# An 8-head attention phase inside a four-phase decoder kernel: one row tile turned before the scores, the keys made in halves, and another order of weight copies in the last batch

## The chip, the cores and the metric

The kernel runs on one core of one Trainium2 chip. The metric is device time in microseconds (us) of one execution; lower is better. The kernel before takes 1964.75 us, the median of 3 runs (1964.06 to 1965.6).

## The reference, cut to what matters

Sixteen sequences of 256 rows with 512 features go through four phases: 16-head cross attention, a ternary gated FFN, 8-head cross attention, a routed FFN. The change is in the third phase. For each of the 16 batches it computes, with the normalised x (normalised twice: once without and once with gain and bias):

```python
q = xn @ Wq ; k, v = split(media @ Wkv)       # 512 -> 8 heads of 64
sim = q k^T / 8, masked ; attn = softmax(sim)
x = x + (attn @ v) @ Wo
```

Everything is float32 in the reference. The kernel multiplies in three terms: each operand is a high part (rounded) and a low part (the rest), and hi*hi, lo*hi and hi*lo are added up in PSUM.

## The kernel before, in words

One program runs the four phases (tags a, b, c, m) one behind the other on five engines: TensorE (PE), ScalarE (ACT), VectorE (DVE), GpSimd (POOL) and the DMA queue of SyncE. Each engine follows an order written out by hand, and semaphores that count finished pieces tie the engines together. No planner sets it: an instruction waits behind all that stand ahead of it on its engine.

`attention_phase` serves phases a (16 heads, QUADS = 4) and c (8 heads, QUADS = 2). Phase c runs from about 1022 to 1608 us of the span. A quad is four heads, so a batch `el` has two quads, q = 0 and q = 1. In iteration `el`, quad q, TensorE (`tensor`, loop at L1212) does for j = 0 to 3:

- only at j = 0: `scores` of the next quad (24 matmuls, L1151), then `probs_v` of the quad before (16 matmuls, L1183);
- `transpose_probs` of head j (4 transposes into one shared bank, L1168), whose result is copied to SBUF by DVE for even j (`probs_out`, L877) and by ACT for odd j (L683); a transpose waits for the copy of the head before it;
- `use_slot`: the units listed in `SLOTS[q][j]` (L247). A unit makes one tile of the next batch, or the output rows of the batch before: `tx0`, `tx1` turn the two tiles of 128 normalised rows (4 transposes each, L1088), `k0`, `k1`, `q0`, `q1` make two feature groups of keys or queries (24 matmuls of 256 columns, L1112; "k0a" and "k0b" are its halves of 12), `v0`, `v1` make 128 rows of values, and `o0`, `o1` the output rows (L1098).

Units alternate between two PSUM banks (`UnitOrder.bank`). `tx0`, `k0` and `o0` use the one, `tx1` and `q0` the other. Before a unit writes its bank (`bank_free`), the unit before it in that bank must be read: ACT copies the high part out of the bank (`hi_of`, for tx at L623), then DVE subtracts it from the bank to get the low part (`lo_of`, for tx at L832). So `k0` waits until DVE has finished `tx0`. The keys come from the stored context and don't need `tx`; `q0` needs both `tx`.

ACT and DVE run `quad_of_8` (L748 and L987): ACT the exponentials of the next quad (`exps`, L675), DVE the scaled and masked scores out of PSUM (`scores_out`, L868), the reciprocals and the norm of the even heads (`recip`, L884 and L890), both the parts of the units slot by slot (`hi_of_slot`, `lo_of_slot`). POOL norms the odd heads and normalises x for the batch after next (`normalise`, L514), whose row tiles `tx0` and `tx1` of one iteration later take as input. In the first iteration that normalise is still running (its rows are below).

In the last batch there is no next batch, and the slots hold work of phase m instead (`beside`): TensorE turns 12 pieces of the shared expert weights (L2557), 2 at a time in quad 0 in slots 0, 1, 2, and 3 at a time in quad 1 in slots 0 and 1; ACT copies the high part of each (`scalar_slot`, L2212), DVE subtracts the low part (`vector_slot`, L2320). A turn waits for the low part of an earlier one that used its bank; `o0` of quad 0, slot 3, waits for the fifth low part. In slots 2 and 3 of quad 1 TensorE turns the first rows of phase m (L2525), after all twelve low parts.

Of the kernel before, what the change touches and what calls it, by code (L numbers as in the profile page):

```python
# [145 lines left out]
def attention_phase(nc, ctx, banks, tag, heads, x_in, ctx_in, mask_in, mask_value, x_out, w_views, q_bias, k_bias,  # L146
# [6 lines left out]
    QUADS = heads // 4  # L153
# [87 lines left out]
    if QUADS == 4:  # L241
        SLOTS = [[["tc0"], ["o0a"], ["o0b"], ["tc1", "o1a", "o1b"]],
                 [["tx0", "v0a"], ["v0b"], ["tx1", "k0a"], ["k0b"]],
                 [["q0a"], ["q0b"], ["v1a"], ["v1b"]],
                 [["k1a"], ["k1b"], ["q1a"], ["q1b"]]]
    else:
        SLOTS = [[["tx0", "tx1"], ["k0a", "k0b"], ["q0a", "q0b"], ["o0a", "o0b"]],  # L247
                 [["o1a", "o1b"], ["k1a", "k1b"], ["q1a", "q1b", "v0a"], ["v0b", "v1a", "v1b"]]]
    BEHIND = ("o0", "o1")
    POOL_NORMS_EVEN = QUADS == 4  # L250

    def finished(parts):

# [11 lines left out]
    def last_batch(el):  # L265
        return isinstance(el.n, int) and el.n == batches - 1
# [11 lines left out]
    def owner(el, u):  # L278

        return el.plus(units.offset(u))  # L280

    def exists(el, u):

        n = el.n
        return not isinstance(n, int) or 0 <= n + units.offset(u) < batches
# [374 lines left out]
    def scalar(act, beside=None):  # L660

        def hi_of_slot(el, q, j):
            for u in finished(SLOTS[q][j]):
                if exists(el, u):
                    hi_of(act, owner(el, u), u)
            if beside and QUADS == 2 and quads_left(el, q):
                beside.scalar_slot(act, quads_left(el, q), j)

        def exps(el, q, h):

            s = slot_of(q, h)
            for t in range(QT):
                act.wait_ge(ttr_done, (el.n * heads + 4 * q + h) * QT + t + 1)
                pr = probs[:, s, h % 2, t]
                nc.scalar.activation(pr, pr, ACT.Exp, bias=negm[:, s, h % 2, t:t + 1], scale=-1.0,  # L675
                                     accum_out=ssum[:, s, QT * (h % 2) + t:QT * (h % 2) + t + 1]) \
                    .then_inc(exp_done, 1)

        def probs_out(el, q, j):

            h = 4 * q + j
            act.wait_ge(pt_done, el.n * heads + h + 1)
            nc.scalar.activation(pT[:, (h // hpg) % 2, h % hpg].rearrange("p t n -> p (t n)"),  # L683
                                 pt_bank[:], ACT.Copy).then_inc(odd_out, 1)

        def attn_hi(el, q):

            act.wait_ge(pv_done, quads_upto(el, q))
            rows = oT[el.par % OT_SETS][:, HI, q * GPQ:(q + 1) * GPQ].rearrange("p g n -> p (g n)")
            if v_bias is None:  # L690
                nc.scalar.activation(rows, o_bank[:, 0:GPQ * SEQ], ACT.Copy).then_inc(othi_done, 1)
            else:
                nc.scalar.activation(rows, o_bank[:, 0:SEQ], ACT.Identity, bias=cols[:, BV, q:q + 1]).then_inc(othi_done, 1)

        def attn_hi_before(el, q):
            if q > 0 or has_before(el):
                attn_hi(*quad_before(el, q))

        start = Element(0, 0, batches)
        if prior:  # L700
            hi_of(act, start, "q0")
            hi_of(act, start, "v0")
            exps(start, 0, 0)
            exps(start, 0, 1)
            hi_of(act, start, "k1")
            exps(start, 0, 2)
            exps(start, 0, 3)
            hi_of(act, start, "q1")
            hi_of(act, start, "v1")
        else:  # L710
            hi_of(act, start, "tc0")
            hi_of(act, start, "tc1")
            hi_of_weight(act, "Wk")
            hi_of(act, start, "tx0")
            hi_of(act, start, "tx1")
            hi_of_weight(act, "Wq")
            hi_of(act, start, "k0")
            hi_of_weight(act, "Wv")
            hi_of(act, start, "k1")
            hi_of(act, start, "q0")  # L720
            hi_of_weight(act, "Wo")
            hi_of(act, start, "v0")
            exps(start, 0, 0)
            exps(start, 0, 1)
            hi_of(act, start, "v1")
            exps(start, 0, 2)
            exps(start, 0, 3)
            hi_of(act, start, "q1")

        def quad_of_16(el, q):  # L730
            ne, nq = next_quad(el, q)
            more = nq > 0 or el.has(1)
            if more:
                exps(ne, nq, 0)
            attn_hi_before(el, q)
            hi_of_slot(el, q, 0)
            probs_out(el, q, 1)
            if more:
                exps(ne, nq, 1)
            hi_of_slot(el, q, 1)  # L740
            if more:
                exps(ne, nq, 2)
            hi_of_slot(el, q, 2)
            probs_out(el, q, 3)
            if more:
                exps(ne, nq, 3)
            hi_of_slot(el, q, 3)

        def quad_of_8(el, q):
            ne, nq = next_quad(el, q)  # L750
            more = nq > 0 or el.has(1)
            if more:
                exps(ne, nq, 0)
            attn_hi_before(el, q)
            if q > 0 and more:
                exps(ne, nq, 1)
            hi_of_slot(el, q, 0)
            probs_out(el, q, 1)
            if q == 0 and more:
                exps(ne, nq, 1)  # L760
            if more:
                exps(ne, nq, 2)
            hi_of_slot(el, q, 1)
            if more:
                exps(ne, nq, 3)
            hi_of_slot(el, q, 2)
            probs_out(el, q, 3)
            hi_of_slot(el, q, 3)

        def iteration(el):  # L770
            for q in range(QUADS):
                (quad_of_16 if QUADS == 4 else quad_of_8)(el, q)
                if beside and quads_left(el, q):
                    beside.scalar_beside(act, quads_left(el, q))

        run_elements(act, batches, iteration)
        attn_hi(Element(0, batches - 1, batches), QUADS - 1)
# [25 lines left out]
    def mask_bias(dve, el):  # L803

        dve.wait_ge(m_loaded[el.par], el.dma())
        nc.vector.tensor_scalar(mbias[:, el.par], mraw[:, el.par], 0.0, mask_value,
                                ALU.is_equal, ALU.mult).then_inc(mbias_ready, 1)
# [53 lines left out]
    def vector(dve, beside=None):  # L861
# [30 lines left out]

        def lo_of_slot(el, q, j):
            for u in finished(SLOTS[q][j]):
                if exists(el, u):
                    lo_of(dve, owner(el, u), u)
            if beside and QUADS == 2 and quads_left(el, q):
                beside.vector_slot(dve, quads_left(el, q), j)
# [90 lines left out]
        def quad_of_8(el, q):  # L989
            ne, nq = next_quad(el, q)  # L990
            more = nq > 0 or el.has(1)
            if q > 0:
                lo_of_slot(el, q - 1, 3)
            elif has_before(el):
                lo_of_slot(el.plus(-1), QUADS - 1, 3)
            if more:
                scores_out(ne, nq, 0)
                scores_out(ne, nq, 1)
                scores_out(ne, nq, 2)
            probs_out(el, q, 0)  # L1000
            if q == 0:
                lo_of_slot(el, q, 0)
            attn_lo_before(el, q)
            if more:
                scores_out(ne, nq, 3)
            if q > 0:
                lo_of_slot(el, q, 0)
            if q == 0 and el.has(1):
                mask_bias(dve, el.plus(1))
            if more:  # L1010
                recip(ne, nq, 0)
            probs_out(el, q, 2)
            lo_of_slot(el, q, 1)
            lo_of_slot(el, q, 2)
            if more:
                recip(ne, nq, 1)
            if q == 0 and el.has(2):
                row_stats(dve, el.plus(2))
# [114 lines left out]
    def tensor(pe, beside=None):  # L1133

        def use_slot(el, q, j):
            for u in SLOTS[q][j]:
                name = u.rstrip("ab")
                if exists(el, name):
                    use(pe, owner(el, name), u)

        def scores(el, q):
# [70 lines left out]
        def iteration(el):  # L1212
            for q in range(QUADS):
                ne, nq = next_quad(el, q)
                for j in range(4):
                    if j == 0 and QUADS == 2:
                        if nq > 0 or el.has(1):
                            scores(ne, nq)
                        probs_v_before(el, q)
# [1615 lines left out]
```

## Time and profile before

| what | value |
|---|---|
| median of 3 runs | 1964.75 us |
| the profiled execution | 1968.88 us, span 1967.2 us |
| TensorE busy | 1904.2 us, 97% of the span |
| VectorE busy | 1296.6 us, 66% |
| ScalarE busy | 1032.7 us, 52% |
| GpSimd busy | 788.1 us, 40% |
| chain that ended last | PE 89%, DVE 3%, issue 2% |
| phase c, time of one batch in the loop | 35.1 us |

The profile shows one execution. Busy is the time in which an engine had an instruction running; for TensorE the ends of matmuls are modelled, so that starts are the surer measure. In a timeline row the first number is the start, the second the busy time of the merged group, and a bracket gives the idle time ahead of it and what ended it. PEclk is the clock granted to TensorE as a share of 2.4 GHz (0.50 is 1.2 GHz).

### The profile page before, as it was taken

To read this page: it belongs to the slowest core of one execution; us is meant where nothing else is said; L and a number is where in the kernel's file an instruction comes from. 1 tells how busy PE (TensorE), PEld (TensorE's weight loads), DVE (VectorE), ACT (ScalarE), POOL (GpSimd) and SP (SyncE) were. 2 spreads that over 40 slices of the span, in tenths; PEclk is the share of its full clock that TensorE was granted. 3 is DMA by queue.
4 is the path that set the end of the run, shared out by engine and by line. 5 is a ranking of instruction groups with operands and counts; after the bars stand their busy time and mean duration, and the time that the engine had idled before them with its cause. 6 is when DMAs were issued, how large, how long until landed. Compare 5 with 4: busy or idle time off the path is not lost.

```text
span 1967.2 us, 43371 instructions
## 1 busy us (share of the span) xinstructions
PE 1904.2 (97%) x13796; PEld 1459.8 (74%) x13828; DVE 1296.6 (66%) x4001; ACT 1032.7 (52%) x2654; POOL 788.1 (40%) x1446
## 2 busy tenths in 40 slices
PE   6999999999999799999989999999999989999998
PEld 5888888888888544444448888888888867787875
DVE  5777777777776678888865655656556556544475
ACT  5777767776777744644435444444444433222252
POOL 2455445454545855655533221312213122222263
PEclk9999999999999999999999999999999989999999
DMA  6332234222325467756653122121221326321131
GB/s 214 121 134 84 83 103 146 83 83 93 136 100 197 141 152 194 184 129 142 148 120 123 56 87 76 65 97 54 86 76 65 103 85 213 103 87 65 64 129 44
DMA packets 197387, 219.54 MB, mean 112 GB/s; under 512 B 105456, under 2 KB 115696, under 8 KB 197248
## 3 DMA queue, kind: packets, MB, share of 16 engines
q1 hardware_dynamic: 197248, 217.93, 35.6%
q8 instruction: 57, 0.93, 0.2%
q14 instruction: 82, 0.67, 0.1%
HBM read 144.47 MB, written 50.35 MB: 99 GB/s over the span
## 4 chain that ended last, share of the span: by engine, by line
PE 89%; DVE 3%; issue 2%; DMA 1%; POOL 1%; ACT 1%; SPq 1%; POOLq 0%; DVEq 0%; ACTq 0%
PE bank L1112 19%; PE bank L1098 18%; PE bank L2619 13%; PE bank L1820 10%; PE bank L1168 8%; PE bank L1183 6%; PE bank L1835 6%; PE bank L1151 5%; PE bank L1088 2%; DMA b_hqT<-b_hq 1%; PE bank L2525 1%; DVE c_xnT L832 1%; SPq L1379 1%; PE bank L2658 1%; ACT c_xnT L623 0%
## 5 line engine op out<-in xcount | busy, mean ns | idle before, releaser
L550 POOL TENSOR_SCALAR a_probs<-a_probs,a_rinv 128x256 f32<-128x256 f32 x512 | 237.4, 482 | 302.6 <-DVE a_rinv L884 302.6
L675 ACT ACTIVATE a_probs<-a_probs,a_negm 128x256 f32<-128x256 f32 x512 | 254.6, 502 | 113.3 <-DVE a_negm L868 112.7
L550 POOL TENSOR_SCALAR c_probs<-c_probs,c_rinv 128x256 f32<-128x256 f32 x128 | 67.0, 533 | 384.6 <-DVE c_rinv L884 384.6
L868 DVE CUSTOM_DVE_ANT_0 a_probs<-bank,a_mbias 128x256 f32<-128x256 f32 x512 | 191.7, 417 | 6.0 <-PE bank L1151 4.3
L2619 PE MATMUL bank<-m_xnT,m_s 128*128 128x512 f32 x768 | 187.0, 395 | 2.7 <-DVE m_hid L2360 2.7
L877 DVE COPY a_pT<-bank 128x512 f32<-128x512 f32 x128 | 88.2, 689 | 137.0 <-PE bank L1168 136.8
L2619 PEld LDWEIGHTS bank<-m_xnT,m_s 128*128 128x128 f32 x768 | 144.2, 190 | 34.1 <-DVE m_hid L2360 3.3
L675 ACT ACTIVATE c_probs<-c_probs,c_negm 128x256 f32<-128x256 f32 x256 | 127.0, 500 | 72.1 <-DVE c_negm L868 72.1
L1168 PE MATMUL bank<-a_ident,a_probs 128*128 128x128 f32 x1024 | 155.2, 274 | 8.3 <-ACT a_pT L683 4.6
L1168 PEld LDWEIGHTS bank<-a_ident,a_probs 128*128 128x128 f32 x1024 | 122.0, 141 | 26.0 <-issue 8.6
L868 DVE CUSTOM_DVE_ANT_0 c_probs<-bank,c_mbias 128x256 f32<-128x256 f32 x256 | 92.8, 419 | 68.1 <-PE bank L1151 68.1
L1638 ACT ACTIVATE b_hq<-b_hround 128x1024 bf16<-128x1024 f32 x64 | 67.3, 1052 | 125.3 <-POOL b_hround L1565 121.3
L1820 PE MATMUL bank<-b_wg,b_xqT 128*128 128x512 bf16 x502 | 130.1, 379 | 1.5 <-issue 1.0
L1820 PE MATMUL bank<-b_wu,b_xqT 128*128 128x512 bf16 x503 | 130.1, 379 | 1.0 <-DVE b_hid L1734 0.5
L1835 PE MATMUL bank<-b_wd,b_hqT 128*128 128x512 bf16 x499 | 116.8, 383 | 7.5 <-DMA b_hqT<-b_hq 6.5
L2149 POOL TENSOR_TENSOR m_hidT<-m_hid,m_hidT 128x512 fp32r<-128x512 f32 x32 | 41.7, 1304 | 196.0 <-ACT m_hidT L2230 196.0
L683 ACT ACTIVATE a_pT<-bank 128x512 f32<-128x512 f32 x128 | 76.3, 596 | 71.0 <-PE bank L1168 70.2
L1624 ACT ACTIVATE b_gate<-bank,b_xs 128x512 f32<-128x512 f32 x128 | 87.0, 683 | 48.5 <-PE bank L1820 44.1
L1112 PE MATMUL bank<-a_cT,a_wk 128*128 128x256 f32 x768 | 109.2, 293 | 1.5 <-DVE a_wk L784 1.5
L1112 PE MATMUL bank<-a_xnT,a_wq 128*128 128x256 f32 x768 | 107.1, 289 | 0.0
L1734 DVE SCALAR_TENSOR_TENSOR b_hid<-bank,b_xs,b_gate 128x512 f32<-128x512 f32 x128 | 95.5, 747 | 16.1 <-ACT b_gate L1624 12.8
L1098 PE MATMUL bank<-a_wv,a_cT 128*128 128x512 f32 x384 | 104.0, 407 | 1.2 <-DVE a_wv L784 1.2
(284 smaller groups left out, 4341.7 us busy)
## 6 DMA issues: line engine op xcount, KB each, us to landing
kept<-a_cT SPq DMA_DIRECT2D x32, 512.0 KB, 5.4
m_ew<-in_L_ffn_w_dram SPq DMA_DIRECT2D x24, 512.0 KB, 8.6
a_cbuf<-in_ctx_dram SPq DMA_DIRECT2D x16, 512.0 KB, 6.4
a_xbuf<-in_x_dram SPq DMA_DIRECT2D x16, 512.0 KB, 5.8
a_resb<-in_x_dram SPq DMA_DIRECT2D x16, 512.0 KB, 4.2
x<-a_resb SPq DMA_DIRECT2D x16, 512.0 KB, 2.8
b_xbuf<-x SPq DMA_DIRECT2D x32, 256.0 KB, 2.9
b_resb<-x SPq DMA_DIRECT2D x32, 256.0 KB, 3.2
```

The source lines that it names most:

```text
L550: last = nc.gpsimd.tensor_scalar(pr, pr, rinv[:, s, r:r + 1], 0.0, ALU.mult, ALU.add)
L675: nc.scalar.activation(pr, pr, ACT.Exp, bias=negm[:, s, h % 2, t:t + 1], scale=-1.0, accum_out=ssum[:, s, QT * (h % 2) + t:QT * (h % 2) + ...
L868: nc.vector.tensor_tensor_reduce(out=probs[:, s, h % 2, t], in0=s_bank[h][:, t * SEQ:(t + 1) * SEQ], in1=mbias[:, el.par], scale=-sm_scale ...
L1098: last = nc.tensor.matmul(dst[:], src[:, t * P:(t + 1) * P], w[:, b, k], start=(k == 0 and (a, b) == TERMS[0]), stop=(k == KC - 1 and (a, ...
L1112: last = nc.tensor.matmul(dst[:, m * SEQ:(m + 1) * SEQ], w[:, b, k, f * P:(f + 1) * P], xnT[:, a, k] if u[0] == "q" else turned_context(el ...
L1151: last = nc.tensor.matmul(s_bank[h][:, t * SEQ:(t + 1) * SEQ], qT[el.par][r, a, f, t * P:(t + 1) * P], kT[el.par][r, b, f], start=((a, b) ...
L1168: last = nc.tensor.transpose(pt_bank[:, kt * SEQ + t * P:kt * SEQ + (t + 1) * P], probs[:, s, m, t, kt * P:(kt + 1) * P], ident[:])
L1183: last = nc.tensor.matmul(o_bank[c, i * SEQ:(i + 1) * SEQ], vb[:, el.par, kt, g * P + m * hd:g * P + (m + 1) * hd], pT[:, g % 2, m, kt], s ...
L1734: nc.vector.scalar_tensor_tensor(hid[:, el.par, c * DIM:(c + 1) * DIM], u_bank[c % 2][:], xs[:, el.par, 1:2], gate[:, c % 4], ALU.mult, AL ...
L1820: last = nc.tensor.matmul(bank[c % 2][:], xqT[:, el.par, k], w[:, k, c * DIM:(c + 1) * DIM], start=(k == 0), stop=(k == KC - 1))
L1835: last = nc.tensor.matmul(d_bank[:], hqT[:, el.par, k], wd[:, k], start=(k == 0), stop=(k == IK - 1))
L2619: ins = nc.tensor.matmul(bank[:], *operands(a, b, k), start=(k == 0 and (a, b) == TERMS[0]), stop=(k == KC - 1 and (a, b) == TERMS[-1]))
```

## The change

1. Slots: `k0a` moves from slot (0, 1) to slot (0, 0), behind `tx1`; so the transposes of head 1 now stand between the two halves of `k0`.
2. `tx0` leaves slot (0, 0): TensorE turns it ahead of the scores of the next quad, ACT copies its high part ahead of the first exponentials, DVE makes its low part ahead of the first scores. This is for every iteration of phase c that has a next batch (15 of 16).
3. In the last batch, ACT makes the high parts of slot 1 before `exps` of head 2 instead of behind it, and DVE makes the low parts of slot 1 before the reciprocals and the copy of head 2 instead of behind them, in both quads.

```diff
-        SLOTS = [[["tx0", "tx1"], ["k0a", "k0b"], ["q0a", "q0b"], ["o0a", "o0b"]],
+        SLOTS = [[["tx0", "tx1", "k0a"], ["k0b"], ["q0a", "q0b"], ["o0a", "o0b"]],
                  [["o1a", "o1b"], ["k1a", "k1b"], ["q1a", "q1b", "v0a"], ["v0b", "v1a", "v1b"]]]
+    AHEAD = "tx0" if QUADS == 2 else None
...
@@ hi_of_slot on ACT; the same in lo_of_slot on DVE and in use_slot on PE @@
-                if exists(el, u):
+                if exists(el, u) and u != AHEAD:
...
@@ quad_of_8 on ACT @@
+            if q == 0 and exists(el, AHEAD):
+                hi_of(act, owner(el, AHEAD), AHEAD)
             if more:
                 exps(ne, nq, 0)
             attn_hi_before(el, q)
...
             if q == 0 and more:
                 exps(ne, nq, 1)
+            if last_batch(el):
+                hi_of_slot(el, q, 1)
             if more:
                 exps(ne, nq, 2)
-            hi_of_slot(el, q, 1)
+            if not last_batch(el):
+                hi_of_slot(el, q, 1)
             if more:
                 exps(ne, nq, 3)
...
@@ quad_of_8 on DVE @@
+            if q == 0 and exists(el, AHEAD):
+                lo_of(dve, owner(el, AHEAD), AHEAD)
             if more:
                 scores_out(ne, nq, 0)
                 scores_out(ne, nq, 1)
...
+            if last_batch(el):
+                lo_of_slot(el, q, 1)
             if more:
                 recip(ne, nq, 0)
             probs_out(el, q, 2)
-            lo_of_slot(el, q, 1)
+            if not last_batch(el):
+                lo_of_slot(el, q, 1)
             lo_of_slot(el, q, 2)
...
@@ the loop over quads and heads on PE @@
+                    if j == 0 and q == 0 and QUADS == 2 and exists(el, AHEAD):
+                        use(pe, owner(el, AHEAD), AHEAD)
                     if j == 0 and QUADS == 2:
                         if nq > 0 or el.has(1):
                             scores(ne, nq)
```

## Rows read from the trace of the kernel before

**Rows 1.** Section 4 of the page: the chain that ended last, share of the span by engine.
```profile
PE 89%; DVE 3%; issue 2%; DMA 1%; POOL 1%; ACT 1%; SPq 1%; POOLq 0%; DVEq 0%; ACTq 0%
```

**Rows 2.** Windows: busy us of PE, PEld, DVE, ACT, POOL; PEclk, DMA, GB/s; one batch.
```profile
1252.80:1287.90 35.10, 34.67 (x267) 29.64 (x266) 20.52 (x65) 16.68 (x48) 8.48 (x19) 1.00 0.21 76
```

**Rows 3.** Waits of the phase (1030 to 1580): total us, times, longest.
```profile
PE bank L1112 <- DVE c_xnT L832: 5.8, 14, 0.4
```

**Rows 4.** Timeline of that batch, TensorE: start us, us, engine, line, count [idle before].
```profile
1252.82 1.69 PE L1151 MATMUL bank<-c_kT,c_qT 64*128 64x256 f32 x24
...
1256.32 0.66 PE L1168 MATMUL bank<-c_ident,c_probs 128*128 128x128 f32 x4
...
1256.81 1.04 PE L1088 MATMUL bank<-c_ident,c_xn 128*128 128x128 f32 x8
...
1257.85 0.63 PE L1168 MATMUL bank<-c_ident,c_probs 128*128 128x128 f32 x4
...
1258.90 3.13 PE L1112 MATMUL bank<-c_cT_odd,c_wk 128*128 128x256 f32 x24 [0.43 <-DVE c_xnT L832]
...
1261.87 0.60 PE L1168 MATMUL bank<-c_ident,c_probs 128*128 128x128 f32 x4
```

**Rows 5.** Timeline, TensorE, the 16-head phase, where keys are already made in halves.
```profile
54.32 0.60 PE L1168 MATMUL bank<-a_ident,a_probs 128*128 128x128 f32 x4
...
54.68 1.67 PE L1112 MATMUL bank<-a_cT,a_wk 128*128 128x256 f32 x12
...
56.19 0.60 PE L1168 MATMUL bank<-a_ident,a_probs 128*128 128x128 f32 x4
...
56.72 0.98 PE L1151 MATMUL bank<-a_kT,a_qT 32*128 32x256 f32 x24
```

**Rows 6.** Timeline of the same batch as in rows 4, VectorE and ScalarE.
```profile
1258.08 1.29 DVE L832 TENSOR_TENSOR c_xnT<-bank,c_xnT 128x512 fp32r<-128x512 f32 x2 [0.38 <-ACT c_xnT L623]
...
1258.51 0.60 ACT L683 ACTIVATE c_pT<-bank 128x512 f32<-128x512 f32 x1
```

**Rows 7.** Timeline of the phase's first iteration, TensorE and GpSimd.
```profile
1046.62 1.69 PE L1151 MATMUL bank<-c_kT,c_qT 64*128 64x256 f32 x24
...
1048.40 1.52 POOL L514 TENSOR_SCALAR c_xn<-c_xbuf,c_ln 128x512 f32<-128x512 f32 x2 [0.18 <-POOL c_ln L512]
...
1054.33 0.60 PE L1168 MATMUL bank<-c_ident,c_probs 128*128 128x128 f32 x4
```

**Rows 8.** Timeline of the last batch, several engines.
```profile
1575.42 0.60 PE L1168 MATMUL bank<-c_ident,c_probs 128*128 128x128 f32 x4
...
1576.07 0.17 DVE L884 RECIPROCAL c_rinv<-c_ssum 128x4 f32<-128x4 f32 x1
...
1576.42 1.06 ACT L2212 ACTIVATE m_s<-bank 128x512 fp32r<-128x512 f32 x2
...
1577.64 1.27 DVE L2320 TENSOR_TENSOR m_s<-bank,m_s 128x512 fp32r<-128x512 f32 x2
...
1577.87 0.50 ACT L675 ACTIVATE c_probs<-c_probs,c_negm 128x256 f32<-128x256 f32 x1
...
1578.46 1.35 PE L2557 MATMUL bank<-m_ident,m_raw 128*128 128x128 f32 x8 [2.44 <-DVE m_s L2320]
...
1580.50 4.03 PE L1098 MATMUL bank<-c_wo,c_oT 128*128 128x512 f32 x12
...
1592.30 1.80 ACT L2212 ACTIVATE m_s<-bank 128x512 fp32r<-128x512 f32 x3
...
1594.43 0.69 DVE L877 COPY c_pT<-bank 128x512 f32<-128x512 f32 x1 [1.68 <-PE bank L1168]
...
1596.97 1.97 PE L2525 MATMUL bank<-m_ident,m_xn 128*128 128x128 f32 x8 [2.58 <-DVE m_s L2320]
...
1600.65 1.73 PE L1183 MATMUL bank<-c_pT,c_vb 128*64 128x256 f32 x13
```

**Rows 9.** Windows: PEclk (third number from the end) after the last batch's first pause.
```profile
1580.00:1582.00 2.00, 2.00 (x8) 1.48 (x7) 1.94 (x5) 1.04 (x2) 0.58 (x2) 0.50 0.00 0
```

More of the change, by code:

```diff
@@ L894, in lo_of_slot @@
             for u in finished(SLOTS[q][j]):
-                if exists(el, u):
+                if exists(el, u) and u != AHEAD:
                     lo_of(dve, owner(el, u), u)
@@ L1137, in use_slot @@
                 name = u.rstrip("ab")
-                if exists(el, name):
+                if exists(el, name) and name != AHEAD:
                     use(pe, owner(el, name), u)
```

## The prediction, made before the changed kernel ran

> **What bounds the kernel now.** I read the chain that ended last first: TensorE holds 89% of the span [rows 1]. Then one steady batch of the phase: TensorE is busy for 34.67 of 35.10 us at full clock, VectorE for 20.52, ScalarE for 16.68 [rows 2]. So only TensorE's own time counts, and the other engines matter where TensorE waits for them. The waits of the phase name one that comes back: the keys' matmuls wait for the low part of a turned row tile, 14 times, 5.8 us in all [rows 3]. The timeline shows its place [rows 4]: behind the transposes of head 1 (1257.85) `k0` starts at 1258.90, with 0.43 us idle, because `tx0` was turned only at 1256.81 and ScalarE and VectorE had still to read its bank.
>
> The gap is wider than the named wait. In the 16-head phase matmuls start 0.36 us behind such transposes (54.32 to 54.68) [rows 5], here 1.05 behind. So 0.69 us is lost per batch. The 8 transposes of `tx0` and `tx1` take 1.04 us (1256.81 to 1257.85) where two groups of four at 0.36 take 0.72: another 0.32, since the transposes of head 1 wait for VectorE's copy of head 0. This second loss goes too if work stands in between.
>
> **Part 1 and 2, a steady batch (14 of them).** No instruction is added or dropped; they change places, and `k0` is cut in two around the transposes of head 1. Before, from the scores to the transposes of head 2: 1252.82 to 1261.87, 9.05 us [rows 4]. After, the same work, start to start:
> - `tx0` to the scores: 0.53, taken from the transposes that stand ahead of scores in the 16-head phase (56.19 to 56.72) [rows 5]. The tile of the scores is another shape there (32 rows, here 64), so this is bounded: 0.36 (as ahead of plain matmuls, 54.32 to 54.68) to 0.72 (twice that).
> - scores to the transposes of head 0: 3.50, as now (1252.82 to 1256.32).
> - those to `tx1`: 0.49, as now (to 1256.81).
> - `tx1` to `k0a`: 0.36 to 0.49; I take 0.42.
> - `k0a` to the transposes of head 1: 1.51 (54.68 to 56.19, the same 12 matmuls) [rows 5]; half of the 2.97 from 1258.90 to 1261.87 would be 1.48.
> - those to `k0b` 0.36, and `k0b` to the transposes of head 2 1.51.
>
> Sum 8.32, so 0.73 less per batch, 10.2 us in 14 batches. At the least only the named wait goes (0.43, 6.0 us); at the most, with 0.36, 0.36 and 1.48, it is 1.02 (14.3 us).
>
> What covers the moves: `tx0`'s low part. Today both row tiles are turned, copied and subtracted from 1256.81 to 1259.37 (VectorE, 1258.08 + 1.29) [rows 4, 6], 2.6 us for two. `k0a` will start 4.94 us behind `tx0` (0.53 + 3.50 + 0.49 + 0.42), so its bank is free long before. `tx0` stands ahead of the first exponentials on ScalarE and ahead of six score tiles on VectorE. VectorE would have to wait for those scores anyway, and its low part costs 0.4 us of delay there; they feed the normed probabilities of the next quad, which TensorE turns only in quad 1. What is late next is ScalarE's copy of head 1: it ends at 1259.11 (1258.51 + 0.60), 1.26 behind the start of its transposes (1257.85) [rows 4, 6]. The transposes of head 2 wait for it, and now stand only 0.36 + 1.51 = 1.87 behind those of head 1: 0.61 us of room, if ScalarE is free when they end. Ahead of it in its queue stand the high part of the attention and that of `tx1`, both released by TensorE before `k0a`. SP's and POOL's orders are untouched; the semaphores count the same units in the same order.
>
> **The first iteration pays.** There the rows of batch 1 are still being normalised: GpSimd writes both tiles from 1048.40 in 1.52 us [rows 7], the first is ready at 1049.16. Today TensorE does the scores at 1046.62 in that time. Now `tx0` stands ahead of them, and everything queued on TensorE waits behind it until about 1049.2. Then 0.53 + 1.69 (scores) + 0.49 + 0.42 + 1.51 + 0.36 + 1.51 gives 1055.71 for the transposes of head 2, against 1054.33: 1.4 us lost. The pause from some 1046.6 to 1049.2 is 2.6 us. The last batch has two such pauses, 2.44 and 2.58 us [rows 8], and in the window after the first the granted clock is 0.50, 1.2 GHz, for the whole 2 us [rows 9], which costs 1.0 us there and something in the slices beside it. I count 1.4 us for such a fall, 2.8 us in all for this iteration (1.4 without the fall, 3.1 with a longer one). The Trainium skill ("TensorE: Matmul & The Clock Gate", The HAM clock gate) says that the clock is throttled by default and that only activity releases it and the rows agree; were the clock kept through this pause, the 1.4 us would not be lost.
>
> **Part 3, the last batch.** In quad 0 turns 2 and 3 end about when the transposes of head 2 start (1575.42) [rows 8], but ScalarE copies their high parts at 1576.42, behind two exponentials of 0.50, and VectorE subtracts at 1577.64, behind reciprocal, norm and copy (from 1576.07). Turn 4 waits until 1578.46. After: high parts from 1575.45, low part of turn 2 at 1576.1, turn 4 at about 1576.9, turn 5 at 1577.5. What is late next: VectorE's copy of head 2 is queued behind both low parts now. It ended 1.57 behind the reciprocal's start (1576.07 to 1577.64); that start moves to 1577.45, so the transposes of head 3 start at about 1579.1. The fifth low part, which `o0` waits for, needs ScalarE's high part behind four exponentials: 1576.6 + 2.0 + 0.6, and 0.7 on VectorE: 1579.9, against 1580.50. So of the 1.56 us only 0.6 arrives. One pause of 2.44 becomes two of about 1.1 and 1.2; whether the clock holds then I can't read from a row. It is worth the same 1.4 if it does, and I count half, 0.7.
>
> In quad 1 the three high parts of slot 1 end at 1594.10 (1592.30 + 1.80). VectorE now takes them as they come, so that the last low part ends at about 1594.9 instead of behind the copy of head 2 (1594.43) and all three (1596.97). The rows of phase m are turned at 1595.0: 2.0 us earlier, and the pause shrinks from 2.58 to 0.8 us, so the clock holds. VectorE's copy of head 2 then ends near 1596.0, the transposes of head 3 follow, ScalarE's two high parts and copy (three at 0.60) end at 1597.5. `probs_v` starts at 1597.6 instead of 1600.65: 3.0 us. At the least only the 2.0 arrives. All behind it follows TensorE in order. This part gives 0.6 + 0.7 + 3.0 = 4.3 us (2.6 to 5.0).
>
> **Sum.** 10.2 - 2.8 + 4.3 = 11.7 us less: 1968.88 - 11.7 = 1957.2 for the profiled execution. That one lies 4.1 us above the median of the runs, so the median becomes 1964.75 - 11.7 = 1953.0. The ends: 14.3 - 1.4 + 5.0 = 17.9 less (1946.9) and 6.0 - 3.1 + 2.6 = 5.5 less (1959.3).
>
> **Rivals.**
> 1. *Only the named wait is worth something.* The extra 0.69 - 0.43 may be the start of a group that comes anyway, and the cut of `k0` may cost as much as the other gap gives back. Then 6.0 - 2.8 + 4.3 = 7.5 less, 1957.2. Against it: the same 12-matmul halves run at 1.51 in the 16-head phase. The Trainium skill ("TensorE: Matmul & The Clock Gate", Architectural detail: the array is 16× 32×32, not 1× 128×128) says that TensorE's queue can pull weight loads ahead of matmuls in flight; by it, `k0`'s first load would be done in the wait, and this rival would hold. The 1.05 us between the two starts speaks against it.
> 2. *VectorE sets the pace.* If VectorE's chain in quad 1 (scores behind output rows) runs without slack, TensorE waits there for what it gained in quad 0. Then 4.3 - 2.8 = 1.5 less, 1963.2, no change that shows. Against it: VectorE idles 14.6 of 35.1 us, and no wait of TensorE on it stands in quad 1.
> 3. *ScalarE's copy of head 1 comes too late, slower.* Place: the transposes of head 2. Price: each us beyond the room of 0.61, 14 times; from 1.45 us late (0.61 + 11.7/14) the kernel is slower. At 2.0 late it costs 19.5 - 11.7 = 7.8 more: 1972.5. For it: ScalarE has `tx0`, the exponentials moved 0.5 to 1.0 us later, the attention's high part and `tx1` ahead of that copy. Against it: ScalarE is busy for less than half of the batch, and what stands ahead is done before `k0a` ends.
>
> **Chances.** Forecast 0.79, rival 1 0.10, rival 2 0.06, rival 3 0.05. A measurement of this kernel tells no change from one of about 0.2%, 3.9 us. Forecast and rival 1 are faster: 0.89. Same 0.06, slower 0.05. The range from 1946.5 to 1959.5 holds the forecast with its bounds and rival 1; rivals 2 and 3 lie outside.
>
> **What would show it.** The wait of L1112 for `c_xnT` gone from the list; from one batch's scores to the next 34.4 us instead of 35.1; `k0a` at 4.9 behind `tx0`; in the first iteration a TensorE pause of 2.6 us for `c_xn` and a granted clock of 0.50 after it; in the last batch turn 4 waits 1.5 us less, the pauses are about 1 us each, and no low clock follows the turns of quad 1. It would be wrong if the transposes of head 2 waited for ScalarE's `c_pT`, if the batch stayed at 35.1, or if TensorE waited for `c_xn` in more than the first iteration.

## The result, and the profile after

The changed kernel takes 1953.94 us (median of 4 runs, 1953.36 to 1955.26), the kernel before 1965.17 beside it (4 runs, 1964.06 to 1968.79): ratio 0.9941, 95% interval 0.9923 to 0.9958, so by the ratio 11.6 us less (8.3 to 15.1). 11.7 us less, 1953.0, was forecast. Below, "us less" is the ratio's share of the time before, unless medians are named. The profiled execution took 1955.26 us with a span of 1953.5, against 1968.88 and 1967.2; its difference of 13.6 us is what the traces have to account for.

The page after, sections 1 and 4: TensorE is still the bound, with 6 us less of busy time.

```profile
PE 1898.3 (97%) x13828; PEld 1460.2 (75%) x13828; DVE 1295.4 (66%) x4001; ACT 1030.9 (53%) x2654; POOL 788.4 (40%) x1446
...
PE 90%; DVE 3%; issue 2%; DMA 2%; POOL 1%; SPq 1%; ACT 1%; POOLq 0%; DVEq 0%; ACTq 0%
```

**A steady batch.** The same stretch by the same view: one batch from scores to scores, now 34.18 us where it was 35.06 (1251.17 to 1285.35; 1252.82 to 1287.88 before), and the 0.43 us in which TensorE had nothing to do are gone [rows 2].

```profile
1251.10:1285.30 34.20, 34.20 (x266) 29.68 (x264) 20.51 (x65) 16.60 (x49) 8.49 (x19) 1.00 0.22 78
```

The timeline of TensorE in the first quad of that batch, against [rows 4]. The transposes of head 2, the last row here, start 8.26 us behind `tx0`, the first; before, they started 9.05 behind the scores. No row has an idle time in brackets.

```profile
1250.64 0.60 PE L1100 MATMUL bank<-c_ident,c_xn 128*128 128x128 f32 x4
...
1251.17 1.70 PE L1163 MATMUL bank<-c_kT,c_qT 64*128 64x256 f32 x24
...
1254.67 0.66 PE L1180 MATMUL bank<-c_ident,c_probs 128*128 128x128 f32 x4
...
1255.17 0.60 PE L1100 MATMUL bank<-c_ident,c_xn 128*128 128x128 f32 x4
...
1255.52 1.68 PE L1124 MATMUL bank<-c_cT_odd,c_wk 128*128 128x256 f32 x12
...
1257.04 0.60 PE L1180 MATMUL bank<-c_ident,c_probs 128*128 128x128 f32 x4
...
1257.39 1.67 PE L1124 MATMUL bank<-c_cT_odd,c_wk 128*128 128x256 f32 x12
...
1258.90 0.60 PE L1180 MATMUL bank<-c_ident,c_probs 128*128 128x128 f32 x4
```

ScalarE's copy of head 1 and VectorE's low part of `tx0` in the same quad, against [rows 6]. The low part ends at 1252.65, 2.9 us ahead of `k0a`; the copy ends at 1258.27, 0.63 ahead of the transposes that wait for it.

```profile
1251.96 0.69 DVE L839 TENSOR_TENSOR c_xnT<-bank,c_xnT 128x512 fp32r<-128x512 f32 x1 [4.36 <-ACT c_xnT L625]
...
1257.67 0.60 ACT L685 ACTIVATE c_pT<-bank 128x512 f32<-128x512 f32 x1 [1.27 <-PE bank L1180]
```

In the waits of the phase the line of [rows 3] is gone, and one wait of the first iteration is new:

```profile
PE bank L1100 <- POOL c_xn L516: 2.6, 1, 2.6
```

**The first iteration**, against [rows 7]: `tx0` stands at 1048.59, the scores that were free to start before stand behind it, and the clock falls. The window under it shows PEclk 0.55.

```profile
1048.59 0.63 PE L1100 MATMUL bank<-c_ident,c_xn 128*128 128x128 f32 x4 [2.62 <-POOL c_xn L516]
...
1049.14 2.10 PE L1163 MATMUL bank<-c_kT,c_qT 64*128 64x256 f32 x24
...
1056.54 0.60 PE L1180 MATMUL bank<-c_ident,c_probs 128*128 128x128 f32 x4
```

```profile
1050.00:1052.00 2.00, 2.00 (x19) 1.78 (x17) 2.00 (x10) 1.05 (x4) 0.11 (x1) 0.55 0.21 51
```

**The last batch**, against [rows 8]: ScalarE's high parts and VectorE's low parts of slot 1, turn 4, VectorE's copy of head 2, the transposes of head 3 that wait for it, `o0`; then the first rows of the next phase and `probs_v` of quad 1.

```profile
1565.51 1.07 ACT L2226 ACTIVATE m_s<-bank 128x512 fp32r<-128x512 f32 x2
...
1566.15 1.28 DVE L2334 TENSOR_TENSOR m_s<-bank,m_s 128x512 fp32r<-128x512 f32 x2
...
1566.98 1.16 PE L2571 MATMUL bank<-m_ident,m_raw 128*128 128x128 f32 x8 [0.89 <-DVE m_s L2334]
...
1568.32 0.67 DVE L884 COPY c_pT<-bank 128x512 f32<-128x512 f32 x1
...
1569.13 1.08 PE L1180 MATMUL bank<-c_ident,c_probs 128*128 128x128 f32 x4 [0.99 <-DVE c_pT L884]
...
1569.87 4.18 PE L1110 MATMUL bank<-c_wo,c_oT 128*128 128x512 f32 x12
```

```profile
1584.39 1.09 PE L2539 MATMUL bank<-m_ident,m_xn 128*128 128x128 f32 x8 [0.49 <-DVE m_s L2334]
...
1586.83 1.95 PE L1195 MATMUL bank<-c_pT,c_vb 128*64 128x256 f32 x16
```

One pause of 2.44 us has become two of 0.89 and 0.99, and yet the clock fell behind them: `o0` is 4.18 us busy, and the window reads 0.50, as in [rows 9]. In quad 1 the pause of 2.58 is 0.49, and no low clock follows.

```profile
1570.00:1572.00 2.00, 2.00 (x7) 1.61 (x6) 1.97 (x6) 0.60 (x1) 1.06 (x2) 0.50 0.00 0
```

**The account.** Starts of four kinds of matmuls cut each trace into stages: A from the first scores of the phase to those of batch 1, quad 0; B from there to the last scores (the second quad of iteration 0, then the 14 steady iterations); C from there to the first gate matmuls of phase m.

| trace | A | B | C |
|---|---|---|---|
| before | 23.34 | 508.62 | 39.96 |
| after | 26.27 | 496.48 | 36.10 |
| forecast of the difference | +2.8 | -10.2 | -4.3 |
| difference | +2.93 | -12.14 | -3.86 |

Together -13.07 us of the 13.7 by which the spans differ. Ahead of stage A the after trace is 0.72 earlier, and from stage C to the end it took 359.06 against 358.97: nothing came or went there.

The clock differs between the two traces, and the differences nearly cancel. Stage A has no low clock before and one after. Stage C has two before (PEclk 0.50 behind the pause of 2.44 us [rows 9], 0.59 and 0.56 in the two windows from 1596 behind that of 2.58) and one after. What the order alone is worth in each stage is read from the experiments that follow.

### The profile page after: what moved, and what is told of

It is laid out like the page before. It is cut to its first block, busy times and chain, and to the rows that moved or that the text cites. A ratio compares the mean times of both kernels' runs of the same rounds, so it can differ in the third digit from the quotient of the medians.

```text
span 1953.5 us, 43409 instructions
## 1 busy us (share of the span) xinstructions
PE 1898.3 (97%) x13828; PEld 1460.2 (75%) x13828; DVE 1295.4 (66%) x4001; ACT 1030.9 (53%) x2654; POOL 788.4 (40%) x1446
## 4 chain that ended last, share of the span: by engine, by line
PE 90%; DVE 3%; issue 2%; DMA 2%; POOL 1%; SPq 1%; ACT 1%; POOLq 0%; DVEq 0%; ACTq 0%
PE bank L1124 19%; PE bank L1110 18%; PE bank L2633 13%; PE bank L1834 10%; PE bank L1180 9%; PE bank L1195 6%; PE bank L1849 5%; PE bank L1163 5%; PE bank L1100 2%; DMA b_hqT<-b_hq 1%; PE bank L2539 1%; SPq L1393 1%; PE bank L2672 1%; DVE m_hrow L2470 0%; POOL a_probs L552 0%
## 5 line engine op out<-in xcount | busy, mean ns | idle before, releaser
L1748 DVE SCALAR_TENSOR_TENSOR b_hid<-bank,b_xs,b_gate 128x512 f32<-128x512 f32 x128 | 95.4, 746 | 15.5 <-ACT b_gate L1638 11.6
L1124 PEld LDWEIGHTS bank<-a_cT,a_wk 128*128 128x128 f32 x768 | 97.2, 194 | 10.4 <-issue 6.2
```

Source lines behind the costliest of these rows:

```text
L1124: last = nc.tensor.matmul(dst[:, m * SEQ:(m + 1) * SEQ], w[:, b, k, f * P:(f + 1) * P], xnT[:, a, k] if u[0] == "q" else turned_context(el ...
L1748: nc.vector.scalar_tensor_tensor(hid[:, el.par, c * DIM:(c + 1) * DIM], u_bank[c % 2][:], xs[:, el.par, 1:2], gate[:, c % 4], ALU.mult, AL ...
```

## The experiments

All are edits of the changed kernel except the last. "Timed" is a ratio to the kernel before, run beside it on the same chip. The stages A, B, C of every trace stand in a table at the end of this section.

**1. `tx0` ahead, `k0` not cut.**

```diff
-        SLOTS = [[["tx0", "tx1", "k0a"], ["k0b"], ["q0a", "q0b"], ["o0a", "o0b"]],
+        SLOTS = [[["tx0", "tx1"], ["k0a", "k0b"], ["q0a", "q0b"], ["o0a", "o0b"]],
```

> The changed kernel, but with k0 whole again in slot (0, 1); tx0 stays ahead of the scores and the last batch keeps its new order. Theory (both parts are needed): tx1 alone (0.49 us) does not fill the time until VectorE has copied head 0, so TensorE waits for c_pT before the transposes of head 1, which start 1.43 us behind those of head 0. A steady batch then saves 9.05 - (0.53 + 3.50 + 1.43 + 0.36 + 2.97) = 0.26 us, with the 0.08 at v1 some 0.3 (4.5 us in 14). With the first iteration's loss of 2.9 and the last batch's gain of 3.9 the kernel is 5.5 us faster than before (4 to 7). Rival (tx0 ahead is the whole gain, the cut adds nothing): 11 us faster, as the changed kernel.

Timed: 1961.83 us (10 runs) against 1967.36 (22 runs), ratio 0.9973 (0.9963 to 0.9983), 5.3 us less. TensorE in a steady quad 0: `tx1`, the transposes of head 1, `k0`, the transposes of head 2.

```profile
1261.33 0.60 PE L1100 MATMUL bank<-c_ident,c_xn 128*128 128x128 f32 x4
...
1262.37 0.63 PE L1180 MATMUL bank<-c_ident,c_probs 128*128 128x128 f32 x4 [0.44 <-DVE c_pT L884]
...
1262.75 3.12 PE L1124 MATMUL bank<-c_cT_odd,c_wk 128*128 128x256 f32 x24
...
1265.71 0.60 PE L1180 MATMUL bank<-c_ident,c_probs 128*128 128x128 f32 x4
```

`k0` no longer waits, but the transposes of head 1 do, 0.44 us for VectorE's copy of head 0 (`c_pT`). Stage B is 3.1 us shorter than before, 0.22 a batch (0.26 forecast). The rival (`tx0` ahead is the whole gain) falls: the wait for `tx0`'s bank was one of two waits in a row, and taking it away hands most of it to the next.

**2. `k0` cut, `tx0` in its old slot.**

```diff
-    AHEAD = "tx0" if QUADS == 2 else None
+    AHEAD = None
```

(and the three places that put `tx0` ahead taken out)

> The changed kernel, but tx0 is back in slot (0, 0) on all three engines; k0a stays behind tx1 there. Theory (both parts are needed): k0a stands ahead of the transposes of head 1 and waits for tx0's low part, until 2.4 us behind the transposes of head 0; those of head 2 then start 0.26 us later than in the kernel before, 3.7 us lost in 14 batches. The first iteration no longer pauses for c_xn, the last batch gains its 3.9: level with the kernel before (-2 to +2 us). Rival (the cut is the gain, it fills the wait for head 0's copy): 6 us from the batches and 3.9 from the last, 10 us faster.

Timed: 1968.1 us (11 runs), ratio 1.0007 (0.9998 to 1.0016). The turned tiles, then `k0a` with its wait:

```profile
1258.95 1.04 PE L1096 MATMUL bank<-c_ident,c_xn 128*128 128x128 f32 x8
...
1261.04 1.69 PE L1120 MATMUL bank<-c_cT_odd,c_wk 128*128 128x256 f32 x12 [1.05 <-DVE c_xnT L837]
```

`k0a` stands at the place where it must wait longest, 1.05 us, 15 times. Stage B is 5.95 us longer than before, 0.43 a batch where I had said 0.26: `k0a` starts 2.09 us behind the turned tiles, just as `k0` did before (1256.81 to 1258.90 in [rows 4]), which is 2.6 behind the transposes of head 0 and not the 2.4 of my sum. The last batch pays most of it back. So the cut alone loses 6.0 us in stage B, `tx0` ahead alone gains 3.1, and both together gain 12.1. The gain lies in the pair: the half of `k0` fills the time until head 0 is copied, and it can only stand there because `tx0` was read before.

**3. The last batch in its old order**, timed twice.

```diff
-            if last_batch(el):
-                lo_of_slot(el, q, 1)
             if more:
                 recip(ne, nq, 0)
             probs_out(el, q, 2)
-            if not last_batch(el):
-                lo_of_slot(el, q, 1)
+            lo_of_slot(el, q, 1)
```

(the same on ScalarE)

> The changed kernel with the last batch in the order of before. Theory (the two parts add up): the trace's 3.9 us of the last batch go, so it is 7.3 us faster than before (6 to 9), with TensorE pauses of 2.4 and 2.6 us and a granted clock of 0.5 after each. Rival (the gain of the last batch is made up later, by a wait at the start of the next phase that does not move): 11 us faster, as the changed kernel.

Timed: 1956.79 us (5 runs), ratio 0.9943 (0.993 to 0.9956), 11.2 us less than before, which spoke for the rival. The trace did not: stage C took 41.31 us against 36.10, with both old pauses back, and the rest of the run was no shorter. The changed kernel was not timed on that chip, so I ran both on one.

> The changed kernel once more, on the chip of the next three runs, as their yardstick. Both theories: 11 to 13 us faster than before. In its last batch the pauses of about 0.9 and 1.0 us in quad 0 are there again; theory (whether the clock falls after them hangs on where they lie in time, not on their length alone): it may fall in one trace and hold in another with the same pauses.

> The changed kernel with the last batch in the order of before, again, since its first timing (10.6 us faster than before) and its trace (5.2 us more in the last batch than in the changed kernel) do not agree. Theory (part 3 is worth what the traces show): 3.9 to 5.2 us slower than the changed kernel on this chip. Rival (it is made up behind the last batch): level with it, within 1.5 us.

Timed on one chip: changed 1956.25 us (5 runs), ratio 0.994 (0.9927 to 0.9954); without part 3 1958.76 (6 runs), 0.9957 (0.9942 to 0.9971). That is 3.3 us by the ratios, with intervals that overlap; stage C 38.37 against 34.87, 3.5. Both lie a little under the 3.9 to 5.2 expected, and above the rival's 1.5. The timings alone don't settle part 3; the traces show a gain of 3.5 to 5.2 us.

That range is mostly the clock. With the old order stage C took 38.37, 39.96 and 41.31 us in three traces. In all three the clock fell behind the pause of 2.44. Behind the pause of 2.58 it held in the first of them, where the turned rows of phase m are 1.09 us busy instead of the 1.97 of [rows 8]:

```profile
1587.14 1.09 PE L2533 MATMUL bank<-m_ident,m_xn 128*128 128x128 f32 x8 [2.58 <-DVE m_s L2328]
```

It fell in the other two, and in the trace of 41.31 it stayed at 0.50 for longer (every window from 1586 to 1592). So the traces with one fall each, 38.37 and 36.10, differ by 2.3 us, about what the new order is worth; the rest of the 3.5 to 5.2 is how often and how long the clock was low.

**4. The first iteration in its old order.** On each engine `tx0` goes ahead only where there is a batch before:

```diff
+    def ahead(el):
+        return AHEAD if not isinstance(el.n, int) or el.n > 0 else None
...
-            if q == 0 and exists(el, AHEAD):
+            if q == 0 and ahead(el) and exists(el, AHEAD):
...
+            if AHEAD and q == 0 and not ahead(el) and j < 2:
+                slot = (["tx0", "tx1"], ["k0a", "k0b"])[j]
```

> The changed kernel, but the first iteration keeps the order of before (tx0 and tx1 in slot (0, 0), k0 whole), so TensorE has scores to do while GpSimd normalises. Theory (the first iteration pays 1.4 us for the pause and 1.5 for the clock that falls after it): 2.9 us faster than the changed kernel, 14 us faster than before (13 to 15.5), no pause over 1 us near 1046 and a granted clock of 1.00 there. Rival (the pause only moves to the first iteration's later waits, 1.4 us for q0): 1.5 us or less beyond the changed kernel, 11 to 12.7 us faster than before.

Timed: 1951.78 us (6 runs), ratio 0.9921 (0.9908 to 0.9933), 15.5 us less. Stage A is 23.31 us, as before the change. So all that the first iteration cost came back (2.96 us against the first trace of the changed kernel, 1.7 against those in which the clock held), and no later wait took it. Stage C is 34.85 here: the clock held in quad 0 of the last batch, with the same two pauses (0.89 and 0.99 us) after which it fell in the first trace of the changed kernel.

**5. The changed kernel again, looked at for the clock.** Its expectation stands above. First iteration: the pause for `c_xn` is there, and behind it the window has a full clock, where the first trace read 0.55.

```profile
1047.73 0.63 PE L1100 MATMUL bank<-c_ident,c_xn 128*128 128x128 f32 x4 [2.64 <-POOL c_xn L516]
...
1048.28 1.70 PE L1163 MATMUL bank<-c_kT,c_qT 64*128 64x256 f32 x24
```

```profile
1050.00:1052.00 2.00, 2.00 (x18) 2.00 (x19) 2.00 (x13) 1.58 (x5) 0.00 (x0) 1.00 0.63 225
```

In the last batch, the transposes of head 3 behind a pause of 0.99, then `o0` in 3.06 us at full clock:

```profile
1567.01 0.63 PE L1180 MATMUL bank<-c_ident,c_probs 128*128 128x128 f32 x4 [0.99 <-DVE c_pT L884]
...
1567.67 3.06 PE L1110 MATMUL bank<-c_wo,c_oT 128*128 128x512 f32 x12
```

Stage A took 25.01 instead of 26.27 and stage C 34.87 instead of 36.10. The same order, the same pauses, and the fall of the clock comes or not: 1.3 and 1.2 us a fall. What decides it (the place in time, as the expectation has it, or something else) no run here shows.

**6. Another order in quad 0 of the last batch**, on top of number 4.

```diff
             if last_batch(el):
                 lo_of_slot(el, q, 1)
+                probs_out(el, q, 2)
+                lo_of_slot(el, q, 2)
             if more:
                 recip(ne, nq, 0)
...
...
+                if last_batch(el):
+                    hi_of_slot(el, q, 2)
```

(the first part is on VectorE, the second on ScalarE; the same calls further down are left out for the last batch)

> The changed kernel with its first iteration as before (2.9 us), and in quad 0 of the last batch a further order: VectorE makes the low parts of slot 1, then the copy of head 2, then the low parts of slot 2, all ahead of the reciprocals and norms; ScalarE makes the high parts of slot 2 ahead of the exponentials of head 3. Theory (the copy of head 2 behind reciprocal and norm is what is late after the change): the transposes of head 3 and o0 start some 1.1 us earlier relative to turn 4, pauses after turn 4 below 0.5 us, clock at 1.00: 1.1 us less than with the first iteration alone, 15 to 17 us faster than before. Rival (the reciprocals, now later, hold up quad 1 or the first rows of the next phase): 14 us or less, with a wait of TensorE for c_probs or m_xn.

Timed: 1950.72 us (4 runs), ratio 0.991 (0.9895 to 0.9924), 17.7 us less than before, where 15 to 17 was expected, and the fastest of all. By the ratios it is 5.9 us below the changed kernel on the same chip; stages A and C of the two traces give 2.4 of them, and the rest is not explained. `o0` now waits 0.22 us, and nothing else behind turn 4 has a wait in that quad; the reciprocal comes only then:

```profile
1565.49 1.16 PE L2582 MATMUL bank<-m_ident,m_raw 128*128 128x128 f32 x8 [0.88 <-DVE m_s L2345]
...
1566.69 0.63 PE L1191 MATMUL bank<-c_ident,c_probs 128*128 128x128 f32 x4
...
1566.79 1.29 DVE L2345 TENSOR_TENSOR m_s<-bank,m_s 128x512 fp32r<-128x512 f32 x2 [0.25 <-ACT m_s L2237]
...
1567.54 3.02 PE L1118 MATMUL bank<-c_wo,c_oT 128*128 128x512 f32 x12 [0.22 <-DVE m_s L2345]
...
1567.99 0.17 DVE L897 RECIPROCAL c_rinv<-c_ssum 128x4 f32<-128x4 f32 x1
```

Stage C is 34.07 against 34.85 at the same clock, 0.8 us where 1.1 was expected: the low parts of slot 2, the fifth first, now wait for ScalarE's high parts (0.25 us), not behind other work of VectorE.

**7. Extra work at the place with the least room.** Two, then one more copy of head 1 into a spare tile.

```diff
             act.wait_ge(pt_done, el.n * heads + h + 1)
+            if QUADS == 2 and (q, j) == (0, 1) and not last_batch(el):
+                for i in range(2):
+                    nc.scalar.activation(spare[:, i], pt_bank[:], ACT.Copy)
```

> The changed kernel, but in quad 0 of every batch save the last ScalarE copies the turned probabilities of head 1 twice into a spare tile before the copy that counts, 1.1 to 1.2 us more at the place with the least room. Theory (the room there is about 0.6 us, TensorE then waits for it): TensorE waits 0.5 to 0.6 us for c_pT ahead of the transposes of head 2 in 15 batches, 8 us slower than the changed kernel, 3 to 5 us faster than before. Rival (there is more room, because other waits take it up, or VectorE sets the pace anyway): within 2 us of the changed kernel.

> As the run with two extra copies of head 1, with one: 0.55 to 0.6 us more at the same place. Theory (the room is 0.6 us, and the two extra copies went 0.5 us beyond it in each of 14 batches): hardly anything is left of the room, the batches still take 34.15 us (34.15 to 34.25), TensorE does not wait for c_pT there. Rival (each extra copy costs its share, there is no such threshold): 34.4 us a batch, half of the loss of two copies.

With two more: the transposes of head 1, the two spare copies, the copy that counts, the transposes of head 2, and the wait in the list of waits (4.7 us, 14 times).

```profile
1261.10 0.60 PE L1184 MATMUL bank<-c_ident,c_probs 128*128 128x128 f32 x4
...
1261.73 1.09 ACT L688 ACTIVATE c_spare<-bank 128x512 f32<-128x512 f32 x2 [1.27 <-PE bank L1184]
...
1262.71 0.60 ACT L689 ACTIVATE c_pT<-bank 128x512 f32<-128x512 f32 x1
...
1263.45 0.63 PE L1184 MATMUL bank<-c_ident,c_probs 128*128 128x128 f32 x4 [0.34 <-ACT c_pT L689]
```

```profile
PE bank L1184 <- ACT c_pT L689: 4.7, 14, 0.3
```

Stage B is 7.1 us longer than in the changed kernel, 0.51 a batch. With one more copy it is 496.86, 0.03 a batch, and the transposes of head 2 follow without a wait:

```profile
1257.64 0.60 ACT L688 ACTIVATE c_spare<-bank 128x512 f32<-128x512 f32 x1 [1.27 <-PE bank L1184]
...
1258.14 0.59 ACT L689 ACTIVATE c_pT<-bank 128x512 f32<-128x512 f32 x1
...
1258.88 0.63 PE L1184 MATMUL bank<-c_ident,c_probs 128*128 128x128 f32 x4
```

So there is a threshold, but it lies at 0.5 us of extra work and not at the 0.6 worked out. In both traces the transposes of head 2 start 0.14 to 0.15 us behind the end of the copy (1263.31 to 1263.45 with two, 1258.73 to 1258.88 with one). Of the 0.63 between the two in the changed kernel only 0.49 is room. The first spare copy pushes the copy that counts back by 0.50 us (1257.64 to 1258.14) and just fits; two push it back by 0.98 (1261.73 to 1262.71), 0.49 too much, and 0.51 was lost. Each extra copy cost less than the 0.55 to 0.6 of the expectation, so it held although the room was smaller.

The timed runs give less than the traces: 1959.67 us (5 runs), ratio 0.9952 (0.9939 to 0.9965), is by the ratios 2.4 us above the changed kernel of the same chip (1956.25, 0.994), and 3.4 by the medians, where 8 were expected. So I repeated the pair on another chip. The kernel with one copy has a single time, 1953.95 against 1965.44.

> The kernel with two extra copies once more, since its stage of steady batches is 7.1 us longer in the trace and its timing only 2.4 us by the ratios. Theory (the trace's 7.1 us are in the timed runs too, and the first timing was scatter): ratio to the kernel before 0.9975 to 0.9985, 6 to 9 us slower than the changed kernel on this chip. Rival (something in the timed runs takes most of it up): again 2 to 4 us slower.

> The changed kernel as the yardstick of the run before on the same chip: ratio 0.994 to the kernel before, stage B of 496.5 us; both theories.

Two more copies: 1957.89 us (6 runs), ratio 0.996 (0.9948 to 0.9973). The changed kernel: 1953.08 us (5 runs), ratio 0.9935 (0.9922 to 0.9948), against 1966.2 (11 runs). That is 4.9 us by the ratios, 4.8 by the medians, with intervals that just touch, between the theory's 6 to 9 and the rival's 2 to 4; stage B is 503.76 against 496.48, 7.3. The place and the threshold are shown by the traces: stage B is 503.58 and 503.76 in the two with two more copies, and 496.48, 496.50 and 496.48 in the three of the changed kernel. The size is 7.1 to 7.3 us there and 2.4 and 4.9 in the timed runs, where the fastest and slowest run of one kernel lie 2 to 10 us apart. That difference stays open.

**8. Part 3 alone, in the kernel before.**

> The kernel before with only the new order of the last batch. Theory (the parts are independent): a batch takes 35.05 us as before, from the last scores to the first gate matmuls of the next phase 34.9 us where the clock holds in quad 0, 36.1 where it falls, against 39.96 before. Rival (the last batch's gain needs the batches ahead to be shorter): 38 us or more there.

One time, 1960.31 us against 1965.44. Stage B is as before (508.61), stage C 34.84, as in the changed kernel where the clock holds: 5.1 us less than the 39.96 before, which had two low clocks. In this one trace the last batch gains the same without the other parts.

| trace | A | B | C |
|---|---|---|---|
| 1: `tx0` ahead only | 26.77 | 505.48 | 36.16 |
| 2: cut only | 23.76 | 514.57 | 34.86 |
| 3: old last batch | 26.27 | 496.48 | 41.31 |
| 3: old last batch, again | 26.24 | 496.50 | 38.37 |
| 4: old first iteration | 23.31 | 496.49 | 34.85 |
| 5: changed, again | 25.01 | 496.50 | 34.87 |
| 6: other order in quad 0 | 23.36 | 496.48 | 34.07 |
| 7: two more copies | 25.54 | 503.58 | 34.90 |
| 7: one more copy | 25.05 | 496.86 | 34.87 |
| 7: two more copies, again | 26.69 | 503.76 | 34.86 |
| 7: changed, third | 25.00 | 496.48 | 34.90 |
| 8: part 3 alone | 23.33 | 508.61 | 34.84 |

## Why the prediction was right

- *What is lost before is 0.69 and 0.32 us a batch, more than the named wait of 0.43.* Right. Experiments 1 and 2 show the two losses as two waits: taking the first away alone gave 0.22 us a batch, and the cut alone lost 0.43. The reason why 0.69 is more than 0.43 can be read from the rows. The transposes of head 1 are 0.63 us busy (with a modelled end), and where nothing waits the next group starts 0.36 behind their start, so it overlaps them by 0.27. A wait loses this overlap and the idle time behind it: 0.27 + 0.43 = 0.70. In experiment 7 it is the same: 0.15 of overlap (`k0b` is 1.67 busy and takes 1.52 start to start) and 0.34 of idle make the 0.49 us by which those transposes came later.
- *A steady batch saves 0.73.* It saves 0.88. Term by term: `tx0` to the scores 0.53 (0.53 said), to the transposes of head 0 3.50 (3.50), `tx1` 0.50 (0.49), `k0a` 0.35 (0.42 taken, 0.36 was the low end), the halves 1.52 and 1.51 (1.51), the transposes between 0.35 (0.36). That is 0.79. The other 0.09 was not in the sum: `tx0` can start 4.20 us behind the last values' matmuls (1246.44 to 1250.64) where the scores could only at 4.29. Over 14 batches the two make 2.1 us; stage B was better than said by 1.9.
- *The room of 0.61 at ScalarE's copy of head 1.* The distance was 0.63, but 0.14 of it passes between the end of a copy and the start of the transposes that wait for it, which the prediction left out: experiment 7 puts the room at 0.5. No wait stands there in the changed kernel, and rival 3 needed the copy 1.45 us later.
- *The first iteration costs 1.4 us for the pause and 1.4 for the clock.* The pause cost 1.67 (trace 5, no fall), with the fall 2.93. Most of the missing 0.3 is one place: there the transposes of head 1 start 1.76 us behind `k0a` and not 1.51. Experiment 4 gave all of it back. The pause was 2.61 to 2.64 us long in all nine traces that have it, and the clock fell behind it in five (stage A from 26.24) and held in four (to 25.54). So my step "2.44 and 2.58 us make the clock fall, so 2.6 does" is not a rule, and that the profiled execution had the fall is luck.
- *Quad 0 of the last batch: 0.6 us, and half a chance for the clock.* `o0` starts 11.53 us behind the last scores instead of 12.23, 0.70. The clock fell in two traces with these pauses (stage C 36.10, and 36.16 in experiment 1) and held in eight (34.84 to 34.90). The clock held more often than the half chance that I counted, and the profiled execution was one of the two others. Late next was VectorE's copy of head 2, as said, and experiment 6 took 0.8 us of it away.
- *Quad 1: 3.0 us.* From `o0`'s successor `probs_v` to the next `probs_v` it is 12.85 us instead of 16.18: 3.3. With the old order and a clock that held (experiment 3, again) it is 14.87. So 2.0 is the earlier turn, as said, and 1.3 the clock. The step "the pause shrinks, so the clock holds" is not shown: the clock also held behind the old pause of 2.58 us, and fell behind pauses of 0.89 and 0.99 in quad 0.
- *Rival 1* (only the named wait is worth something) is out by 12.1 us in stage B against its 6.0; *rival 2* (VectorE sets the pace) by the batch of 34.18.
- *The sum.* Stages A to C of the profiled executions differ by 13.07 us where 11.7 was forecast: 1.9 more from the steady batches, 0.1 and 0.4 less from the other two stages. The mechanisms are shown. That the timed difference of 11.6 us comes within 0.1 of the forecast is luck: its interval is 8.3 to 15.1, and 1.2 us or more hang on each fall of the clock.

The Trainium skill ("TensorE: Matmul & The Clock Gate", Architectural detail: the array is 16× 32×32, not 1× 128×128) has weight loads pulled ahead of matmuls in flight. In the trace before that did not happen in the old wait. The first weight load of `k0` starts at 1258.90, together with its first matmul, behind 0.66 us without a load:

```profile
1258.90 2.93 PEld L1112 LDWEIGHTS bank<-c_cT_odd,c_wk 128*128 128x128 f32 x24 [0.66 <-issue]
```

## What to carry to other kernels

A wait that the profile names is one link. Ask which wait would end last if it were gone, and compare start to start with a place where the same instructions run free, since the named idle time leaves out the overlap that is lost too: here the difference was 0.69 against a named 0.43, and two edits that alone gave +0.22 and -0.43 us a batch gave 0.88 together. A step that is moved ahead in a loop meets its first iteration too, where its input is not yet made: leave that iteration as it was.

## What the runs showed that I had not expected

A fall of the clock behind a pause is not fixed by the pause. The pause of 2.6 us in the first iteration was followed by a granted clock of 0.55 in one execution and of 1.00 in another of the same kernel, and pauses of 0.89 and 0.99 us by 0.50 in one and 1.00 in another. Over all traces the clock fell behind the first in five of nine, behind the pair in two of ten, behind the old pause of 2.44 us in three of three and behind that of 2.58 in two of three. Most falls cost 1.2 to 1.6 us (1.6 is stage C of the trace before, 39.96, against the 38.37 of experiment 3), the long one of experiment 3 cost 2.8. The Trainium skill ("TensorE: Matmul & The Clock Gate", The HAM clock gate) says that the number of slow matmuls at the start of a kernel varies from run to run; these rows agree, and show the same behind pauses inside a kernel. A part of the 2 to 10 us by which runs of one kernel differ here can come from that, but some of it lies elsewhere: phase c began between 1020.5 and 1023.8 us over the traces of all these kernels, with the same work ahead of it.
